# One retention layer with an FP4 side branch on one core: in groups two and three, k is turned to token-major by DMA instead of TensorE, and the first states are computed ahead of the weight tile's scales

## The reference, cut to what matters

```python
q = heads((x @ Wq + bq) * scaling); k = heads(x @ Wk + bk); v = heads(x @ Wv + bv)   # 16 heads of 64
ret = einsum('bhid,bhjd->bhij', q, k) * D          # D[i,j] = exp(decay * (i - j)), causal
ret = ret / clip(abs(ret.sum(-1, keepdims=True)), 1.0, None)
attn = einsum('bhij,bhjd->bhid', ret, v)
g = groupnorm(attn) * gn_w + gn_b
attn_branch = (silu(x @ Wg + bg) * g) @ Wo + bo
ffn_branch = dequantized(quantize_nvfp4(x)) @ dequantized(quantize_nvfp4(weight)).T + bias
out = x_in + attn_branch + ffn_branch
```

## Time and profile before

| | us |
|---|---|
| median of 3 runs | 2092.87 |
| lowest and highest of them | 2090.34, 2092.93 |
| the profiled execution, its own time | 2086.01 |
| its span, from first to last instruction | 2083.9 |

### The profile page before, as it was taken

The page is one execution under the profiler, slowest core; times in us unless marked ns, Lnnn a source line. Parts: engine busy times, 40 slices in busy tenths (PEclk is TensorE's granted clock), DMA queues, the critical chain, the costliest instruction groups (busy, mean ns, idle before and its releaser), DMA issues.

```text
span 2083.9 us, 53458 instructions
## 1 busy us (share of the span) xinstructions
PE 2006.4 (96%) x18850; PEld 1112.0 (53%) x18894; DVE 1658.7 (80%) x4411; ACT 692.3 (33%) x1359; POOL 893.8 (43%) x634
## 2 busy tenths in 40 slices
PE   5899989999999999999999999999999999999999
PEld 3444555555555555555555555555555555555544
DVE  7677689988899898888988888777777777777832
ACT  6666632322232323223233223233323233323310
POOL 2223333332343343555544555544555554455530
PEclk9999999999999999999999999999999999999999
DMA  8888624333434334445444345434345434435552
GB/s 328 281 295 304 212 92 131 106 126 110 112 121 141 123 105 124 119 140 151 121 127 131 115 137 148 122 105 129 112 124 146 131 99 138 113 105 146 150 168 110
DMA packets 272090, 302.15 MB, mean 145 GB/s; under 512 B 204656, under 2 KB 205808, under 8 KB 271856
## 3 DMA queue, kind: packets, MB, share of 16 engines
q1 hardware_dynamic: 272000, 300.98, 47.6%
HBM read 207.33 MB, written 43.52 MB: 120 GB/s over the span
## 4 chain that ended last, share of the span: by engine, by line
PE 57%; DVE 33%; issue 5%; ACT 2%; DMA 1%; DVEq 0%; SPq 0%; POOL 0%; ACTq 0%; POOLq 0%
PE mm L1588 27%; PE mm L1605 9%; PE mm L1498 6%; PE tp L1498 6%; PE mm L1507 2%; DVE state L1305 2%; DVE gst L1319 2%; DVE xa L1080 2%; PE four L1663 2%; DVE xa L1088 2%; DVE xa L1075 2%; PE four L1676 1%; DVE wo L1193 1%; DVE xa L1087 1%; DVE xm L1082 1%
## 5 line engine op out<-in xcount | busy, mean ns | idle before, releaser
L1588 PE MATMUL mm<-xnT,wring 128*128 128x512 f16 x4776 | 1063.2, 380 | 12.0 <-ACT kT L853 6.4
L1588 PEld LDWEIGHTS mm<-xnT,wring 128*128 128x128 f16 x4776 | 458.3, 98 | 546.0 <-issue 7.5
L1605 PE MATMUL mm<-wring,xnT 128*128 128x256 f16 x2688 | 302.8, 273 | 5.3 <-DVE res L1447 5.1
L915 ACT ACTIVATE work<-four,gs 128x64 f32<-128x64 f32 x512 | 158.1, 414 | 401.1 <-DVE gs L1332 401.1
L1605 PEld LDWEIGHTS mm<-wring,xnT 128*128 128x128 f16 x2688 | 261.1, 98 | 50.9 <-DVE res L1447 14.4
L682 POOL TENSOR_TENSOR yT<-gn,gate 128x512 f32 (+1 forms) x64 | 83.8, 1310 | 349.0 <-ACT gn L926 240.1
L1498 PE MATMUL mm<-wo,yT 128*128 128x512 f16 x960 | 214.1, 380 | 2.5 <-POOL yT L687 2.2
L659 POOL TENSOR_TENSOR qparts<-qT,qparts 128x512 f16<-128x512 f32 x64 | 78.8, 1232 | 237.8 <-ACT qT L853 237.8
L695 POOL TENSOR_TENSOR nparts<-work,nparts 128x512 f16<-128x512 f32 x41 | 47.4, 1157 | 266.0 <-ACT nparts L901 266.0
L1319 DVE BATCH_NORM_STATS2 gst<-four 128x6 f32<-128x64 f32 x512 | 73.5, 216 | 99.0 <-PE four L1676 97.6
L1498 PEld LDWEIGHTS mm<-wo,yT 128*128 (+1 forms) x960 | 90.8, 98 | 110.7 <-POOL yT L687 2.7
(11 more groups left out here) (226 smaller groups left out, 2980.9 us busy)
## 6 DMA issues: line engine op xcount, KB each, us to landing
wring<-parts SPq DMA_DIRECT2D x252, 512.0 KB, 4.8
xt<-in_x SPq DMA_DIRECT2D x34, 512.0 KB, 4.9
out<-res SPq DMA_DIRECT2D x32, 512.0 KB, 3.0
parts<-wo SPq DMA_DIRECT2D x28, 512.0 KB, 5.8
res<-in_x SPq DMA_DIRECT2D x28, 512.0 KB, 3.6
ftile<-in_w_f SPq DMA_DIRECT2D x12, 512.0 KB, 4.5
parts<-wring SPq DMA_DIRECT2D x8, 512.0 KB, 8.2
probs<-in_x SPq DMA_DIRECT2D x5, 512.0 KB, 4.8
```

The lines of the kernel that those rows point to most:

```text
L915: last = nc.scalar.activation(work[:, c * P + h * HD:c * P + (h + 1) * HD], ao[h][:, c * VW:c * VW + HD], ACT.Identity, bias=gs[:, 1, g:g ...
L1588: last = MM(mm[n % 2][:], wring[:, slot, wj, k, :], xnT[:, parity, xj, k, :], start=(j == 0), stop=(j == 3 * KT - 1))
L1605: last = MM(out[:, c], xnT[:, parity, xj, k, tokens], wring[:, 1::2, wj, k, :], start=(n == 0), stop=(n == 3 * KT - 1))
```

## The change

In SECOND and THIRD the eight PE transposes of a body are gone. SP issues `move_k(0)` and `move_k(1)`, POOL runs `join_k(0)` and `join_k(1)`, and ACT runs `scale_k` where `decay_k` was, though later in its order. On DVE, `states(0)` stands ahead of `f_scales`. The tables that count semaphore steps and bank uses follow suit.

```diff
@@ SP, a QUANTIZE body
                     load_slice(0, 0)
+                    move_k(0)
                     load_slice(0, 2)
                     load_gates()
                     move_x_parts()
+                    load_slice(1, 0)
+                    move_k(1)
                     w("xq_ready", 1)
                     load_x(1)
-                    load_slice(1, 0)
                     load_v(0)
@@ POOL
                 def join_k(u):
-                    w("t0_full", u)
+                    w("t0_full", bank_uses(phase)["u0"][1] if u else 0)
                     w("k_moved", u + 1)
...
                     if phase != FIRST:
                         bias_v(1)
+                        join_k(0)
                     split(3, kT[:], kparts)
                     split(4, qT[:, 1], qparts)
                     decay_q(1)
+                    if phase != FIRST:
+                        join_k(1)
                     if phase in QUANTIZE:
                         add_biases()
@@ ACT
-                    decay_k(0)
                     evacuate_v(1)
+                    scale_k(0)
                     evacuate(1, 0)
                     evacuate(0, 3)
-                    decay_k(1)
                     evacuate(1, 2)
+                    scale_k(1)
                     normalize(0)
@@ DVE
                     mask_scores(0)
                     quantize_half(xt, 1)
+                states(0)
+                if phase in QUANTIZE:
                     f_scales()
-                states(0)
@@ PE
-                    if phase == MIDDLE:
-                        w("kn_ready", u + 1)
-                    else:
-                        for which in ("kv" if phase == FIRST else "k"):
+                    if phase == FIRST:
+                        for which in "kv":
                             b, n = uses[f"{which}{u}"]
                             w(f"t{b}_free", n)
-                    if phase != FIRST:
+                    else:
+                        w("kn_ready", u + 1)
                         w("v_ready", 2)
...
-                if phase != MIDDLE:
+                if phase == FIRST:
                     transpose_kv(0, "k", kT, 0)
...
-                if phase != MIDDLE:
+                if phase == FIRST:
                     transpose_kv(1, "k", kT, 0)
```

More of the change, by code:

```diff
@@ L81 @@
     "mm1_full": (1, 4, 5, 5, 6, 1), "mm1_free": (1, 4, 5, 5, 6, 1),
[2 rows of a table removed]
-    "k_joined": (0, 0, 0, 0, 2, 0), "kn_ready": (0, 0, 0, 0, 2, 0),
[2 rows of a table added]
+    "k_joined": (0, 0, 2, 2, 2, 0), "kn_ready": (0, 0, 2, 2, 2, 0),
     "nhi_ready": (1, 0, 0, 0, 2, 0), "n_split": (1, 0, 0, 0, 2, 0), "n_joined": (1, 0, 0, 0, 2, 0), "gn_ready": (1, 0, 0, 0, 2, 0),
@@ L94 @@
     "xqf_ready": (0, 0, 1, 1, 0, 0), "xqf_moved": (1, 0, 1, 1, 0, 0), "f_loaded": (0, 0, 1, 1, 0, 0),
-    "k_moved": (0, 0, 0, 0, 2, 0), "n_moved": (2, 0, 0, 0, 4, 0),
+    "k_moved": (0, 0, 2, 2, 2, 0), "n_moved": (2, 0, 0, 0, 4, 0),
     "xq_moved": (1, 0, 1, 1, 1, 0), "x_moved": (1, 2, 2, 2, 2, 0),
@@ L131, in bank_uses @@
     elif phase in QUANTIZE:
-        t0, t1 = ("g1", "k0", "u0", "u1"), ("k1", "g0")
+        t0, t1 = ("g1", "u0", "u1"), ("g0",)
     else:
```

## The result

| kernel | median us | lowest to highest | runs |
|---|---|---|---|
| before | 2092.20 | 2087.59 to 2093.48 | 13 |
| changed | 2087.94 | 2086.40 to 2089.45 | 13 |

The ratio is 0.9982, with a 95% interval of 0.9975 to 0.9990. The changed kernel is faster by 0.18%, 3.8 us by the ratio, where +1.0 us was forecast. That is less than the 0.2% which the prediction set as its bound, and still told apart from nothing.

What follows compares the result with a forecast made beforehand. A loop through POOL's train and DVE's `group_norm(0)`, not PE alone, was taken as the bound. Seven intervals at +0.1 (+0.7) and the first SECOND body (+0.3) made +1.0 on the 2092.87 median: 2093.9 us, range 2085.5 to 2101.

Steps and rivals of the forecast that it cites:

- What bounds the body: SECOND body: a loop through PE, POOL's train, DVE's `group_norm(0)` and `group_norm(1)`, and ACT's evacuation of k, not PE alone.
- One sign: PE at the next `project(0, 2)`: its wait for ACT would grow from 0.61 to about 2.2 us.
- `group_norm(0)` starts 0.6 us earlier: DVE, later SECOND bodies: round trip of 0.90 goes, `join_k(0)` adds 0.8, `split(3)` gives back 0.4; start near 421.4.
- the 0.4: DVE ahead of `group_norm(0)`: `split(3)` falls mostly on `mask_scores(0)`, giving back 0.4 of the 0.83 us it costs.
- It ends at 427.5: POOL's train, with `join_k(1)` as fourth member: starts 0.93 earlier, takes 1.24 more, ends 0.3 us later than before.
- `group_norm(0)` ends 0.1 later: DVE behind the train: one more 0.2 us step slips through, so it ends 0.1 us later; bounds -0.6 and +0.6.
- Seven intervals at +0.1: SECOND bodies after the first, and THIRD bodies: each 0.1 us longer, +0.7 us in all.
- The first SECOND body ... I take +0.3: First SECOND body: PE's 3.56 wait goes, `f_scales` steps get caught, `group_norm(0)` ends 0.9 to 2.9 later; net +0.3 us.
- To which I add the same: Whole kernel: the +1.0 us was added to the median of 2092.87, 6.9 above the profiled execution, giving 2093.9.
- the faster one: Rival, chance 0.27: the train doesn't hold `group_norm(0)`'s end; -0.6 to -1.0 a body, 2085 to 2088 us.
- The slower one: Rival, chance 0.2: the tail of `f_scales` is caught by `split(4)`; 1.15 us a body in seven, 2102 us.
- k did not come late: Rival, chance 0.05: DMA transposes over 7.6 us hold ACT's `evacuate(1, 0)`; at 10 us, +7, 2101 us.

Runs made afterwards that it cites:

- PE kept busy: The changed kernel with eight unread transposes of the identity on PE where those of k had been; 2094.05 us, ratio to before 1.0014.
- `join_k(1)` twice: The changed kernel with an extra addition like `join_k(1)` ahead of it on POOL, in the train, into a scratch tile; 2095.86 us, ratio to before 1.0026.
- `add_biases` out of the train: The changed kernel with `add_biases` moved on POOL to behind `split(3)`, held until x is quantized; 2074.45 us, ratio to before 0.9923.
- the control: The kernel before with the first SECOND body written out on PE instead of looped, same instructions; 2091.46 us, ratio to before 0.9999.
- the run that filled the wait: The kernel before, first SECOND body written out on PE, with 24 identity transposes inside its wait ahead of `attend_earlier(0)`; 2090.80 us, ratio to before 0.9995.
- `join_k(0)` twice: The changed kernel with an extra addition like `join_k(0)` ahead of it on POOL, before the train, into a scratch buffer; 2096.21 us, ratio to before 1.0027.

## Why the prediction was wrong, by its own steps

- *What bounds the body*: right. PE is freed of 0.93 us a body and the body is not; the runs with PE kept busy, with `join_k(1)` twice and with `add_biases` out of the train show that POOL's train and DVE's `group_norm(0)` set it. That the loop closes through ACT is read from the traces alone. One sign was wrong: the wait of `project(0, 2)` did not grow to 2.2 us. It stayed at 0.61, and 0.98 us are spent ahead of the transposes of the normed output.
- *"`group_norm(0)` starts 0.6 us earlier"*: it starts 0.97 earlier. The round trip of 0.90 is gone as reckoned, `join_k(0)` cost L1088 its 0.8, and `split(3)` gave back more than the 0.4: it lies now on `mask_scores(0)`, the step that took 1.26 at 410.11 takes 0.43 now, at 411.37.
- *"It ends at 427.5"*: the train ends at 427.76 on its own clock, 427.42 on that of before. One more step slips through, as said. "`group_norm(0)` ends 0.1 later" became 0.06 earlier.
- *"Seven intervals at +0.1"*: this term was mis-sized, by 0.3 us a body in SECOND and 0.2 in THIRD, and it had the wrong sign. They are -0.19 in SECOND and -0.07 in most of THIRD, -0.9 in all where +0.7 was forecast. Of the 0.19, 0.06 come up to the end of `group_norm(0)` and 0.13 behind it, where I had written that nothing changes: POOL's `gate_y(0)` now begins somewhat earlier than DVE's first state, which it stretches by less.
- *"The first SECOND body ... I take +0.3"*: the step that failed, twice over. In traces at full clock it is -1.0. Three steps of `f_scales` were caught, at 0.91, 0.95 and 0.79 us over their free length, as forecast, and `group_norm(0)` starts 1.45 us later on the body's clock. But it ends only 0.62 later and not 0.9 to 2.9: a step of its own that had been caught, at 1.06, was free now (0.24). With DVE's later waits for PE shrunk from 0.26 and 1.57 to none and 0.24, that makes -0.97, and in each trace one further DVE step is stretched by POOL's `gate_y(0)`, by 0.7 to 0.8 us. And the wait of 3.56 us had a second price that I didn't ask for: of the three traces with this wait (3.56 us in two of before, 3.41 in the control), two show the clock falling behind it, and the first interval 1.5 to 1.7 us longer. The traces with that fall sum to 496.76 and 496.57 over the eight intervals, against 492.96 and 492.91 of the two traces of after: 3.7 us, where the medians differ by 3.9 to 4.3.
- *What stays open*: that these figures agree does not show that this fall fills the gap, and the run that filled the wait, 0.7 us under its control and not told apart from it, does not show it either. At one and the same reported clock the changed kernel is still about 3 us faster: at 0.998, 2086.9 on average in eleven executions against 2089.9 in ten; at 0.996, 2088.7 in five against 2092.1 in seventeen. Its mean clock over 24 executions is 0.9969, against 0.9965 over 75 of before, which by my estimate (0.0004 of 2088 us) is 0.8 us. The means differ by 3.5 us (2087.3 against 2090.9); with the 1.9 us of the eight intervals that leaves 0.8 in no place that a trace shows.
- *"To which I add the same"*: the profiled execution of before lay 6.9 us under the median. I noted that and went on, though its clock of 0.999 said that it was an execution in which the clock had hardly fallen. Over 75 runs of before beside these experiments, the ten at 0.999 took 2086.9 on average, and the thirty at 0.995 or 0.996 took 2092.3.
- *The rivals*: the faster one put its gain in all bodies (-0.6 to -1.0 each), and its condition, `group_norm(0)` ending before 429.7, did not come about. The measured median lies in its 2085 to 2088, and in the stated range, by luck: half of the gain seen in the traces is in the first body. The slower one, that the train catches `f_scales`, did not come about in the later bodies: L1072 ends at 421.18, 0.5 us ahead of `split(4)`. k did not come late; the DMA transposes landed within 6.7 us.

The Trainium skill ("TensorE: Matmul & The Clock Gate", Part 1) says that PE's clock drops to half once it has been idle for long enough, and comes back only after it has been busy again. The 3.56 us of the earlier trace rows were thus a reason to ask for the clock. The traces agree in part: there is a fall behind that wait in two of three, behind one of 4.07 us in the run that moves k alone, where the 24 matmuls took 7.63, and behind one of 2.79 us (`join_k(1)` twice, interval 65.09). But the length of the wait does not decide it here. Falls also stand behind waits of 1.92 us (the first trace of the changed kernel, at 783) and 1.74 (`join_k(1)` twice, at 746), and behind two of 1.10 and 1.04 with work between them (changed kernel, at 251), while waits of 3.56 us (first trace of before) and 2.46 (PE kept busy, at 768) passed without one.

## What to carry to other kernels

A wait of PE can cost more than its length when the clock falls behind it; price it at both levels, and before a single profile is taken as typical, compare its own time and clock with the median. Where DVE runs many tiny steps beside a back-to-back train on POOL, the end of the train is the end of those steps: take an instruction out of the train before you take work from anyone else. Work taken from an engine that is not the bound is worth nothing until the bound is moved: k by DMA gained next to nothing beside the swap, and 0.6 to 0.95 us in each body but the first once `add_biases` had left the train. The best version here has both and takes 2074.45, 0.77% under before.

## What the hardware showed that I had not expected

The same kernel, with the same wait of 3.56 us, keeps the full clock in one execution and loses it in others; a loss took 1.5 to 1.7 us of PE's time or twice that (3.4 in the run that moves k alone, over 6 us at half clock), and one that fell where PE was not the bound left the body as long as it was. When one such place was removed another turned up in MIDDLE, in single traces. And DVE steps of 0.17 us that begin under a POOL instruction and read no PSUM lasted until it ended, within 0.04 us, up to 2.28 us (`join_k(0)` twice).
